# A four-layer conditioned transformer stack: padding-mask tables built on ScalarE, operand buffers moved by 32 bytes, layer 0's folded bias added by VectorE

## The reference

```python
# layer 0, attention
V = h @ v_w + v_b
attn = softmax(scores)
x = x_in + ((attn @ V) @ proj_w + proj_b)
# layer 3, attention
mask = padding_mask[:, None, :] & padding_mask[:, :, None]
attn = jnp.where(mask[:, None, :, :], attn, -1000000000.0)
attn = softmax(attn)
```

## Time and profile before

| | |
|---|---|
| median of 3 runs | 2184.35 us (2183.79 to 2184.51) |
| profiled execution | 2190.35 us, its span 2188.6 us |
| TensorE matmul busy | 2071.5 us, 95% |
| TensorE weight load busy | 1680.1 us, 77% |
| VectorE busy | 1338.6 us, 61% |
| ScalarE busy | 981.0 us, 45% |
| GpSimd busy | 429.3 us, 20% |
| mean granted TensorE clock | 0.987 of 2.4 GHz |

### The profile page before, as it was taken

The page is one execution under the profiler, slowest core; times in us unless marked ns, Lnnn a source line. Parts: engine busy times, 40 slices in busy tenths (PEclk is TensorE's granted clock), DMA queues, the critical chain, the costliest instruction groups (busy, mean ns, idle before and its releaser), DMA issues.

```text
span 2188.6 us, 44429 instructions
## 1 busy us (share of the span) xinstructions
PE 2071.5 (95%) x15652; PEld 1680.1 (77%) x15652; DVE 1338.6 (61%) x2536; ACT 981.0 (45%) x1577; POOL 429.3 (20%) x385
## 2 busy tenths in 40 slices
PE   6998999999999999999999999997999999998998
PEld 5786887777777788877777777775788777787887
DVE  5865655776766656654544555456666677775664
ACT  2434554444444333334444444443444555454443
POOL 3532001322221111101111121123300322210000
PEclk9999999999999999999999999999999999999999
DMA  6000000000000000000000000000000000000000
GB/s 216 20 15 8 8 7 11 16 8 14 7 7 11 20 10 19 12 13 7 7 6 5 5 0 5 5 1 13 8 5 5 16 6 10 5 5 1 29 19 29
DMA packets 18405, 33.38 MB, mean 15 GB/s; under 512 B 1298, under 2 KB 12050, under 8 KB 17810
## 3 DMA queue, kind: packets, MB, share of 16 engines
q1 hardware_dynamic: 18322, 32.25, 4.5%
HBM read 28.06 MB, written 4.19 MB: 15 GB/s over the span
## 4 chain that ended last, share of the span: by engine, by line
PE 79%; DVE 9%; issue 7%; POOL 2%; ACT 2%; DMA 0%; DVEq 0%; SPq 0%; ACTq 0%; POOLq 0%
PE psum L588 21%; PE psum L589 20%; PE psum L590 20%; PE psum L685 4%; PE psum L698 3%; PE psum L630 2%; PE psum L717 2%; DVE xn L1074 2%; PE psum L783 2%; PE psum L731 2%; PE psum L674 1%; PE psum L523 1%; DVE h_lo L1095 1%; PE psum L705 1%; DVE pb L1150 1%
## 5 line engine op out<-in xcount | busy, mean ns | idle before, releaser
L588 PE MATMUL psum<-h_hi,w_lo 128*128 128x512 f32 x1120 | 465.2, 415 | 10.7 <-DVE h_lo L1095 6.3
L590 PE MATMUL psum<-h_hi,w_hi 128*128 128x512 f32 x1120 | 446.3, 398 | 0.0
L589 PE MATMUL psum<-h_lo,w_hi 128*128 128x512 f32 x1120 | 445.5, 398 | 0.0
L1202 DVE TENSOR_TENSOR hid_lo<-hid,hid_hi 128x512 fp32r<-128x512 f32 x256 | 200.9, 786 | 268.8 <-ACT hid_hi L949 268.5
L949 ACT ACTIVATE hid_hi<-hid 128x512 fp32r<-128x512 f32 x256 | 161.8, 632 | 224.5 <-PE psum L590 135.1
L588 PEld LDWEIGHTS psum<-h_hi,w_lo 128*128 128x128 f32 x1120 | 212.9, 190 | 64.4 <-issue 11.3
L590 PEld LDWEIGHTS psum<-h_hi,w_hi 128*128 128x128 f32 x1120 | 212.4, 190 | 51.3
L1291 POOL TENSOR_TENSOR rstd<-ms,half_t 128x4 f32<-128x4 f32 x64 | 66.3, 1036 | 920.8 <-DVE ms L1069 475.1
L589 PEld LDWEIGHTS psum<-h_lo,w_hi 128*128 128x128 f32 x1120 | 213.0, 190 | 42.5
L1147 DVE TENSOR_REDUCE mx<-psum 128x8 f32<-128x512 f32 x192 | 132.4, 690 | 163.1 <-PE psum L674 108.9
L944 ACT ACTIVATE hid<-psum,vec 128x512 f32<-128x512 f32 x192 | 132.0, 687 | 203.4 <-PE psum L590 201.6
(11 more groups left out here) (139 smaller groups left out, 3646.2 us busy)
## 6 DMA issues: line engine op xcount, KB each, us to landing
stage<-in_w_dram SPq DMA_DIRECT2D x24, 256.0 KB, 2.7
stage<-in_w_dram SPq DMA_DIRECT2D x8, 512.0 KB, 3.6
out_dram<-xres SPq DMA_DIRECT2D x8, 512.0 KB, 2.9
xres<-in_x_dram SPq DMA_DIRECT2D x1, 3584.0 KB, 18.5
modw_mod<-in_modw_dram SPq DMA_DIRECT2D x2, 1536.0 KB, 13.6
stage<-in_w_dram SPq DMA_DIRECT2D x8, 384.0 KB, 3.3
stage<-in_w_dram SPq DMA_DIRECT2D x8, 192.0 KB, 2.3
modw_film<-in_modw_dram SPq DMA_DIRECT2D x1, 1024.0 KB, 7.4
```

The lines of the kernel that those rows point to most:

```text
L588: nc.tensor.matmul(dst, s_lo, m_hi, start=start and j == 0, stop=False)
L589: nc.tensor.matmul(dst, s_hi, m_lo, start=False, stop=False)
L590: ins = nc.tensor.matmul(dst, s_hi, m_hi, start=False, stop=stop and j == len(pairs) - 1)
L1202: nc.vector.tensor_tensor(hid_lo[:, slot, :], hid32[:, slot, :], hid_hi[:, slot, :].bitcast(F32), ALU.subtract).then_inc(sem["hid"], 1)
```

## The change

Four things are edited.

1. The tables are made by ScalarE, in the stages `up` 3 to 6 of the first block of layer 2's MLP, each in front of that chunk's GELU. `mask_qs` is now mask times plus 4294967296, `mask_ks` is mask minus 1 on its row, for which VectorE makes the small buffer `no_seq` (minus the identity's first two columns) at the start. `prepare_mask` goes; GpSimd waits for the tables (`mask_made`) before it cuts the first block of layer 3.
2. `no_seq` is placed ahead of `mx`, and a line in front of `at_hi` brings the running address to 32 mod 64.
3. Stage `bias` goes, with its semaphore and the wait on it.
4. Layer 0's value rows leave PSUM by VectorE, which adds `vo_bias` on the way. ScalarE no longer takes part in stage `v` of layer 0.

```diff
--- before.py
+++ after.py
@@ -96,7 +96,7 @@
         return [nxt("stats"), prev("divide"), own("q", 0), own("q", 1), own("k", 0), nxt("norm"), own("k", 1), prev("probs_t"),
-                own("bias"), nxt("turn"), prev("pv"), prev("back"), nxt("split"), own("scores"), own("v", 0), own("v", 1),
+                nxt("turn"), prev("pv"), prev("back"), nxt("split"), own("scores"), own("v", 0), own("v", 1),
                 own("exp"), own("share")]
@@ -164,7 +164,7 @@
     if layer == 0:
-        c.update(q=2, k=2, v=2, w_full=1, out_rows=0, biased=1)
+        c.update(q=2, k=2, v=2, w_full=1, out_rows=0)
     if layer in (1, 3):
@@ -251,12 +252,14 @@
         half_t = place("half_t", [P, TILES], F32)
+        no_seq = place("no_seq", [P, 2], F32)
         mx = place("mx", [P, 2, SEQ], F32)
...
         pt = place("pt", [P, 2, BLK], F32)
+        at[0] += 32 - at[0] % 64
         at_hi = place("at_hi", [P, 2, BLK], F32R)
@@ -806,11 +809,26 @@
+            def mask_table(n):
+                g = n % 2
+                if n < 2:
+                    nc.scalar.activation(mask_qs[:, :, g, :], mask_rows[:, :, :], ACT.Copy, scale=MASKED).then_inc(mask_made, 1)
+                else:
+                    nc.scalar.activation(mask_ks[:, :, g, :], mask_rows[:, :, :], ACT.Identity, bias=no_seq[:, g:g + 1],
+                                         scale=col("ident", g)).then_inc(mask_made, 1)
             def stage_of(ph, s, k, b):
...
                     table_part(k)
+                if PHASES[ph] == ("mlp", 2) and s == "up" and 3 <= k < 7 and is_first(b):
+                    if k == 3:
+                        act.wait_ge(mask_loaded, 16)
+                        act.wait_ge(mask_made, 1)
+                        act.wait_ge(sem["x_done"], n_at("x_done", ph, 0, 1))
+                    mask_table(k - 3)
                 if is_first(b) and (s, k) == ("k_out", 0):
@@ -822,19 +840,15 @@
                         nc.scalar.activation(h_of(ph, b)[0][:, m, :], hm[:, m, :], ACT.Copy).then_inc(sem["h_hi"], 1)
-                elif (s in ("q", "k", "v") if layer in (0, 2) else s in ("q_out", "k_out", "v_out")) and kind == "attn":
+                elif (s in ("q", "k") or s == "v" and layer == 2 if layer in (0, 2) else s in ("q_out", "k_out", "v_out")) and kind == "attn":
                     bank, at = a_slot(ph, s[0], k, b)
...
                         act.wait_ge(full, at + 1)
-                        if s == "v":
-                            nc.scalar.activation(v0_sb[b % 2][:, 2 * k:2 * k + 2, :], src.rearrange("p (t d) -> p t d", d=D),
-                                                 ACT.Copy).then_inc(fre, 1)
-                        else:
-                            act.wait_ge(sem["s_full0"], n_at("s_full0", ph, b, 0))
-                            dst = q0_sb if s == "q" else kk
-                            nc.scalar.activation(dst[:, k, :], src, ACT.Identity, bias=col(f"{s}0", k)).then_inc(fre, 1)
+                        act.wait_ge(sem["s_full0"], n_at("s_full0", ph, b, 0))
+                        dst = q0_sb if s == "q" else kk
+                        nc.scalar.activation(dst[:, k, :], src, ACT.Identity, bias=col(f"{s}0", k)).then_inc(fre, 1)
                         act.wait_ge(fre, at + 1)
@@ -983,6 +997,7 @@
                                       col(name, 0, DC).unsqueeze(2).to_broadcast([P, DC, P])).then_inc(vo_cols, 1)
+            nc.vector.tensor_scalar(no_seq[:, :], col("ident", 0, 2), -1.0, None, ALU.mult).then_inc(mask_made, 1)
             full = 8 * batch
@@ -1121,6 +1136,17 @@
                     dve.sem_inc(sem[f"a_free{bank}"], 1)
+                elif s == "v" and layer == 0:
+                    if k == 0 and is_first(b):
+                        dve.wait_ge(vo_cols, 3)
+                    bank, at = a_slot(ph, s, k, b)
+                    dve.wait_ge(sem[f"a_full{bank}"], at + 1)
+                    nc.vector.tensor_tensor(v0_sb[b % 2][:, 2 * k:2 * k + 2, :], acc_a[bank].rearrange("p (t d) -> p t d", d=D),
+                                            vo_bias[:, :].unsqueeze(1).to_broadcast([P, 2, D]),
+                                            ALU.add).then_inc(sem[f"a_free{bank}"], 1)
+                    dve.wait_ge(sem[f"a_free{bank}"], at + 1)
+                    dve.sem_inc(sem["v"], 1)
                 elif s == "scores" and layer == 0:
@@ -1219,8 +1245,6 @@
                         last = 3 if layer in (1, 3) else 1
-                        if layer == 0:
-                            dve.wait_ge(sem["biased"], n_at("biased", ph, b, 1))
                         dve.wait_ge(sem["w_full"], n_at("w_full", ph, b, last))
@@ -1265,17 +1289,10 @@
-            def prepare_mask():
-
-                pool.wait_ge(mask_loaded, 16)
-                for g in range(2):
-                    nc.gpsimd.tensor_scalar(mask_qs[:, :, g, :], mask_rows[:, :, :], -MASKED, None, ALU.mult).then_inc(prepared, 1)
-                    nc.gpsimd.tensor_scalar(mask_ks[:, :, g, :], mask_rows[:, :, :], 0.0, col("ident", g), ALU.is_equal, ALU.mult).then_inc(prepared, 1)
-                prepares[0] += 4
-                pool.wait_ge(prepared, prepares[0])
-
             def mask_of_block(ph, c, b):
+                if c == 0 and is_first(b):
+                    pool.wait_ge(mask_made, 5)
                 pool.wait_ge(sem["s_full1"], n_at("s_full1", ph, b, -2 if c == 0 else 0))
@@ -1311,20 +1328,11 @@
                     mask_of_block(ph, k, b)
-                elif s == "bias":
-                    if is_first(b):
-                        pool.wait_ge(vo_cols, 3)
-                    pool.wait_ge(sem["normed"], n_at("normed", ph, b, 1))
-                    xs = xres[:, bass.ds(b * TILES, TILES), :]
-                    nc.gpsimd.tensor_tensor(xs, xs, vo_bias[:, :].unsqueeze(1).to_broadcast([P, TILES, D]),
-                                            ALU.add).then_inc(sem["biased"], 1)
                 elif s == "share":
...
                             prepare_attention()
-                        if PHASES[ph + 1:ph + 2] == [("attn", 3)]:
-                            prepare_mask()
                     split_next(ph, b)
```

More of the change, by code:

```diff
@@ L213, in build @@
         t1_ready = ctx.enter_context(nc.semaphore("t1_ready"))
+        mask_made = ctx.enter_context(nc.semaphore("mask_made"))
         mask_cleared = ctx.enter_context(nc.semaphore("mask_cleared"))
```

## The result

| | before | after |
|---|---|---|
| median (range), runs | 2184.43 us (2183.79 to 2187.27), 4 | 2161.45 us (2160.25 to 2161.95), 4 |
| profiled execution, its span | 2190.35, 2188.6 us | 2160.96, 2159.2 us |
| mean granted clock | 0.987 | 0.994 |

After over before is 0.9892, 95% interval 0.9874 to 0.9909: 23.0 us faster. The forecast was 2153 us, in a range of 2143 to 2184. The two profiled spans differ by 29.4 us, 6 more than the medians; that much the profiled execution of before stands above its median, and part of it is layer 1's attention, where TensorE ran at a granted clock of 0.97 before and 0.99 after, with the same work.

A forecast was written before the change was run, and what follows sets the result against it. TensorE was taken as the bound, carrying 79% of the chain that ended last. Profiled 2190.35 us - 11.3 - 1.5 - 19 = 2158.5, with the median 6.0 lower: 2152.5, said as 2153 us, range 2143 to 2184.

The forecast's parts named there:

- Part 1: Layer 2's MLP, block 0: mask tables moved from GpSimd to ScalarE shorten the stretch to layer 0's, 11.3 us saved.
- Rival D: Layer 2's MLP, block 0: ScalarE's table operations delay the GELUs, +8 us, 2161 us; chance 0.05.
- Part 2: Layer 0's attention: GpSimd's bias adds go, VectorE adds the bias while draining value rows; 1.5 us saved.
- Rival C: Layer 0's attention: next `q` waits the full 2 us a block for VectorE's drain, +14 us, 2168 us; chance 0.09.
- Part 3: Buffers from `mx` on move to 32 mod 64, so `h` and weights agree and matmuls start closer; 19 us saved.
- the pair, not the grid: Matmul spacing: a streamed and stationary operand that disagree modulo 64 cost 4.8 to 5.8 ns, whichever is off the grid.
- rival A: Matmul spacing: an operand off the 64-byte grid costs 4.8 ns once, also when both are off; 2177 us; chance 0.28.
- B: Matmul spacing: each operand off the 64-byte grid costs its own 4.8 ns, `h` at about 238 ns; 2206 us; chance 0.13.

The follow-up runs named there:

- e1: Kernel before with mask tables made by ScalarE, later buffers moved by a whole 64 bytes, bias as before: 2171.39 us, ratio 0.9936.
- e3: Kernel before with only layer 0's bias moved to VectorE on the way out of PSUM, tables and buffers unchanged: 2185.93 us, ratio 1.0000.
- e2: Kernel before with only 32 bytes left free ahead of `mx`: 2178.84 us, ratio 0.9959.
- e8: Kernel after without the 32-byte shift (tables by ScalarE, bias by VectorE, buffers at their old place modulo 64): 2171.02 us, ratio 0.9929 to before.
- e4: Kernel before with 32 free bytes ahead of `xn` and 32 more ahead of `mx`, everything at 0 mod 64: 2174.64 us, ratio 0.9951.
- e12: Kernel after with 192 bytes ahead of `mx`, late GpSimd clears and layer 0's value products ahead of the scores: 2154.2 us, ratio 0.9855 to before.
- e5: Kernel after with 64 more bytes ahead of `mx`, `h` and weights equal modulo 512: 2153.15 us, ratio 0.9851 to before.
- e9: Kernel after with 320 more bytes ahead of `mx`, `h` 256 bytes (mod 512) from the weights: 2150.93 us, ratio 0.9838 to before.
- e7: Kernel after with GpSimd's clears of `kx` and `vb` held until VectorE has normalised the next block: 2156.99 us, ratio 0.9861 to before.

## Why the prediction was right, and where it was not

**What bounds the kernel.** Right. The gain that the traces show is a standstill removed, clock given back, or closer matmuls.

**Part 1: forecast -11.3 us, measured -14.0 us (interval 11 to 17).** The mechanism was right in each step. The stretch was to come down to layer 0's 28.2 us, and with part 1 alone (e1) it took 27.9, at the forecast clock of 0.94: 11.7 us saved against 11.3. The 26.3 us in after go with a clock of 1.00 in that one execution. TensorE's standstill for `xn` is 2.9 us instead of 8.3, and that for `hid_lo` (3.4 us) is gone. Of the rest up to 14.0 us, I estimate 2 us for the layout of e1, whose move by 64 bytes I had taken for neutral. Four ScalarE operations of 1.90 to 2.08 us were taken at 2 us, and they were hidden. Rival D falls with it: the idle time of ScalarE before the GELUs is used up, but TensorE waits neither for `hid_lo` nor for ScalarE there.

**Part 2: forecast -1.5 us, measured 0.0, within 2 us.** Right in mechanism and within the error in size. The wait for `xn` was replaced by the one for the value drain (at most 1.7 us a block against 2.0 worked out), and the chain that had the 2.4 us of the bias on it gave back about as much as the drain takes. Rival C falls: not +14 us, as e3 shows. The prediction has no term for the clock here, and the traces show one: 0.96 to 1.00 from 60 to 152 us. The medians show nothing of it, so the sum came out right without that term: luck. One detail was wrong: `xn` was to come at 344 ns each, and the mean is 506, because one of the four now lies beside GpSimd's division of `pb` (in one block `xn` starts at 91.04 and the four take 1.92 us, `pb` at 90.97 for 1.04 us).

**Part 3: forecast -19 us, measured -9.0 (e2), about 8 (e8 against after).** This is the step that failed, in size only. The prediction had three terms: 4.8 ns for each of 3360 matmuls of `h` over weights, 5.8 ns for 384 value products, about 1 ns for 2208 of `hid` and `at`. Measured as means over the traces: 3.3 ns, 0.7 ns, and 0.2 (`hid`) and 1.0 ns (`at`, 672 matmuls); 3.3 x 3360 = 11.1 us, 0.3 us, and 0.3 and 0.7 us. That is 12.4 us, somewhat above the 9.0 measured and just outside its interval of 6 to 12.

The reading "the pair, not the grid" was right against rivals A and B: e4, with everything on the grid, has after's spacing, e8, with only `h` 32 bytes from its place in e4, has 233 ns, and nothing rose to 238. What was wrong is the word "agree". I took it as agree modulo 64, because `at` over weights and `h` over weights differed in that; they also differed modulo 256 (0 against 96), and the rows could not tell the two apart. e12 does: its 128 bytes agree modulo 64, and it has 232.6 ns. The change brought `h` from a distance of 96 to one of 64, so from 233.5 to about 230 ns. In the MLPs only a distance of 0 or 256 brings the 226.5 ns, and e5 and e9 show the missing half: 8 and 11 us below after (9 and 12 by the ratios). There `h` over weights stands 4.9 ns below before (228.6 against 233.5), the 4.8 that were forecast. But of the step from after to e5 at least as much comes from `hid` over weights as from `h`: 3.9 ns in 1536 matmuls, 6.0 us, against 1.6 ns in 3360, 5.4 us, though the distance of `hid` didn't change. The prediction had put about 1 ns on that. Had the distance been written down in bytes for each pair instead of "agrees", the doubt would have been visible in front.

The weighing of the Trainium skill's rule ("TensorE: Matmul & The Clock Gate", Part 2, two independent read ports, so that loading the next weights takes nothing from the running matmul) came out against what the prediction drew from it, that the place of the operands changes nothing: the place of the two to each other is worth up to 7 ns of 233. Whether the two reads take bandwidth from each other, or something else does it, no run here shows. One slip stands in that weighing: a change without any effect of the place gives 2184.35 - 12.8 = 2171.6 us, not rival A's 2177; e1 and e8, where `h` stayed at 233 ns, have 2171.

**The sum.** Part 1 gave 3 us more, part 2 1.5 less, part 3 10 less: 2153 + 8.5 = 2161.5. The misses partly cancel. The time lies just outside the forecast's own spread (2144 to 2160) and on rival D's 2161, and D isn't what happened. The range, drawn for rival A, held the time for a reason that was not A: that part is luck.

## What to carry to other kernels

When a slower and a quicker row of matmuls differ by where their operands lie, write down the distance in bytes of each pair and vary it on purpose: here `h` a multiple of 256 bytes from the weights is worth some 17 to 20 us of 2184 (9 in the change, 8 to 11 more in e5 and e9), and costs one line. Look at neighbouring runs too, since they move with it. An engine that does only clears and tables can still be the one that stops TensorE, by stretching VectorE's normalise (four took 11.53 us in before and 1.38 us in e7); move such work to an engine whose idle time the timeline shows at that place, or behind the operation that it would hold. Where a removed wait sits in front of a bank that another engine must empty, work out who comes to the bank late, and expect about nothing.

## What the runs showed of the hardware

- In the MLPs of this kernel, matmuls of 128x512 float32r (`h` over weights, a new weight tile each) follow each other in 226.5 ns when streamed and stationary operand lie a multiple of 256 bytes apart in SBUF (0 and 256 tried), in 229.6 to 230.4 ns at 64 bytes, in 232.6 at 128, in 233.0 at 32 and in 233.5 at 96. At 64 bytes, whether both are on a 64-byte grid or both off it changes nothing (229.8 ns, the median over the stretches, in e4 and in after).
- In the attention of layers 1 and 2 the step from 64 bytes to 0 brings nothing for `h` over weights: 229.2 and 229.5 ns in after, 229.1 and 229.2 in e5.
- The effect does not stay within its own matmuls: `hid` over weights, whose distance is 0 in before, after and e5, showed a median spacing of 230.2, 231.2 and 226.6 ns. It lies between runs of `h`, and goes with them.
- For weights streamed in tiles of 256 columns over a stationary `h` it is the other way round: 123.6 ns in after, 126.9 in e5 and 125.4 before (mean spacing). About 480 matmuls have this form.
- ScalarE turns 128x2048 uint8 into bf16 in 1.90 us with a constant factor and in 2.08 us with factor and bias from columns; GpSimd took 5.38 and 7.66 us for its two forms, with VectorE active.
- Two GpSimd clears in a row, of 3.5 and 1.9 us, stretch the VectorE normalise beside them from 0.4 to 5.4 us (before and after), but leave a two-input subtraction at 0.69 us (e7).
